# A masked-softmax graph layer on one core: ring transfers of one unit instead of two around the turn between row groups

## What is computed

```python
h = jnp.maximum(_layernorm(x, axis=-1), 0.0)
H = h @ W_fc + b_fc
s_src = H @ w_att[:d]
s_dst = H @ w_att[d:]
scores = s_src[:, None] + s_dst[None, :] + b_att
scores = jnp.where(adj > 0, scores, -1e9)
alpha = jax.nn.softmax(scores, axis=1)
out = x + alpha @ H
```

## Time and profile before

| | us |
|---|---|
| median of three runs | 186.04 |
| lowest, highest | 185.82, 186.31 |
| the profiled execution's own time | 186.24 |
| its span, first to last instruction | 184.3 |
| PE busy | 160.3 |
| DVE busy | 124.9 |
| ACT busy | 79.6 |
| mean rate of the transfers | 389 GB/s |

### The profile page before, as it was taken

One profiled execution on the slowest core, in us unless ns is written; L12 is line 12 of the kernel. 1 busy time (PEld: TensorE's weight loads), 2 busy tenths in 40 slices (PEclk: granted clock), 3 DMA queues, 4 the chain that ended last, 5 costly groups with the idle time before them and its releaser, 6 DMA issues.

```text
span 184.3 us, 2691 instructions
## 1 busy us (share of the span) xinstructions
PE 160.3 (87%) x866; PEld 115.3 (63%) x866; DVE 124.9 (68%) x360; ACT 79.6 (43%) x232; POOL 10.7 (6%) x33
## 2 busy tenths in 40 slices
PE   0639859989499999989899999999999998999970
PEld 0326638666386867656668667686786775887750
DVE  0995696947999556788865569496594624459931
ACT  2567894999395052222251422442224424021020
POOL 2103601000130020000000000000000000000000
PEclk9999987999969999999999999999999999999995
DMA  5999999999999999999999999999999999998212
GB/s 144 410 439 432 412 443 420 434 420 430 427 430 432 412 441 411 441 420 428 420 422 424 427 427 424 422 427 423 425 424 427 437 431 427 411 398 329 76 60 59
DMA packets 8369, 71.63 MB, mean 389 GB/s; under 512 B 929, under 2 KB 1698, under 8 KB 3490
## 3 DMA queue, kind: packets, MB, share of 16 engines
q1 hardware_dynamic: 7776, 71.18, 92.3%
q10 hardware_dynamic: 578, 0.26, 0.5%
HBM read 69.34 MB, written 2.10 MB: 388 GB/s over the span
## 4 chain that ended last, share of the span: by engine, by line
DMA 59%; PE 23%; DVE 10%; issue 2%; ACT 2%; SPq 1%; DVEq 0%
DMA ring<-adj 59%; PE bank L844 9%; PE bank L850 8%; DVE mask L514 5%; PE bank L868 3%; PE bank L892 2%; PE bank L882 1%; DVE low L537 1%; ACT mask L456 1%; DVE mask L523 1%; ACT weighted L363 1%; SPq L271 1%; DVE x_sb L639 1%; DVE x_sb L646 1%; SPq L277 0%
## 5 line engine op out<-in xcount | busy, mean ns | idle before, releaser
L514 DVE TENSOR_SCALAR mask<-ring 128x1024 fp32r<-128x1024 int32 (+2 forms) x69 | 63.1, 934 | 41.6 <-DMA ring<-adj 37.1
L844 PE MATMUL bank<-mask,high 128*128 128x512 f32 x256 | 80.7, 418 | 11.0 <-DVE mask L514 6.3
L850 PE MATMUL bank<-mask,low 128*128 128x512 f32 x256 | 76.3, 401 | 0.0
L844 PEld LDWEIGHTS bank<-mask,high 128*128 128x128 f32 x256 | 47.8, 196 | 31.1 <-DVE mask L514 12.9
L850 PEld LDWEIGHTS bank<-mask,low 128*128 128x128 f32 x256 | 49.8, 194 | 11.1
L456 ACT ACTIVATE mask<-ring,half_steep 128x512 fp32r<-128x512 int32 x43 | 28.9, 718 | 62.1 <-DMA ring<-adj 60.6
L868 PE MATMUL bank<-mask,w_cols 128*32 128x512 bf16 x256 | 19.7, 392 | 2.3 <-ACT lines L422 2.3
L868 PEld LDWEIGHTS bank<-mask,w_cols 128*32 128x32 bf16 x256 | 5.9, 94 | 13.1 <-issue 8.7
L363 ACT ACTIVATE weighted<-relu,w_over_std 128x128 f32<-128x128 f32 x32 | 10.1, 391 | 4.7 <-DVE w_over_std L608 4.5
L374 ACT ACTIVATE relu<-x_sb,neg_mean 128x128 f32<-128x128 f32 x32 | 9.8, 388 | 3.2 <-DVE neg_mean L546 3.2
L389 ACT ACTIVATE high<-x_sb,neg_mean 128x128 fp32r<-128x128 f32 x24 | 9.3, 387 | 0.0
(11 more groups left out here) (85 smaller groups left out, 67.7 us busy)
## 6 DMA issues: line engine op xcount, KB each, us to landing
ring<-adj SPq DMA_DIRECT2D x18, 2048.0 KB, 17.1
ring<-adj SPq DMA_DIRECT2D x16, 1536.0 KB, 12.9
ring<-adj SPq DMA_DIRECT2D x3, 1024.0 KB, 9.3
out<-x_sb SPq DMA_DIRECT2D x7, 256.0 KB, 13.8
x_sb<-x SPq DMA_DIRECT2D x1, 1024.0 KB, 20.7
ring<-adj SPq DMA_DIRECT2D x4, 256.0 KB, 16.2
x_sb<-x SPq DMA_DIRECT2D x2, 256.0 KB, 3.8
x_sb<-x SPq DMA_DIRECT2D x1, 512.0 KB, 10.1
```

The source lines that it names most:

```text
L514: nc.vector.tensor_scalar(mask[:, n % MASKS, 0:cols], ring[:, n // 2 % RING, begin:begin + cols], 0.0, None, ALU.is_gt).then_inc(masks_rea ...
L844: nc.tensor.matmul(bank[:, b, :], high[:, t, :], mask[:, n % MASKS, cols], start=(t == 0), stop=False)
L850: last = nc.tensor.matmul(bank[:, b, :], low[:, t, :], mask[:, n % MASKS, cols], start=False, stop=(t == T - 1))
```

## The change

Eight pairs, 10 to 17 (units 20 to 35; the last six pairs of group 0 and the first two of group 1), come as two transfers of one unit each instead of one of two units. Each half has a semaphore of its own, and the wait for a unit is on its half. The slots of the ring, the condition under which SP may refill a slot, and the order of the work on every engine stay as they are. Both halves of a pair are issued behind the same `slot_free`.

```diff
+HALVED = range(10, 18)
...
+        half_landed = [[sem(f"half_landed{c}_{i}") for i in range(2)] for c in range(RING)]
...
             if pair == 0:
                 engine.wait_ge(first_landed[n], 16)
+            elif pair in HALVED:
+                engine.wait_ge(half_landed[pair % RING][n % 2], 16 * ((pair - HALVED.start) // RING + 1))
             elif n == LAST - 1:
                 engine.wait_ge(next_to_last_landed, 16)
             else:
-                engine.wait_ge(pair_landed[pair % RING], 16 * (pair // RING + (pair % RING > 0)))
+                whole = [p for p in range(1, pair + 1) if p % RING == pair % RING and p not in HALVED]
+                engine.wait_ge(pair_landed[pair % RING], 16 * len(whole))
...
                 if pair >= RING:
                     slot_free(pair)
-                sp.dma_start(ring[:, pair % RING, 0:cols], adj_g[g][t0 // (2 * step)]).then_inc(pair_landed[pair % RING], 16)
+                if pair in HALVED:
+                    for i in range(2):
+                        half = slice(i * cols // 2, (i + 1) * cols // 2)
+                        sp.dma_start(ring[:, pair % RING, half], adj_g[g][t0 // (2 * step)][:, half]).then_inc(half_landed[pair % RING][i], 16)
+                else:
+                    sp.dma_start(ring[:, pair % RING, 0:cols], adj_g[g][t0 // (2 * step)]).then_inc(pair_landed[pair % RING], 16)
```

## The result

The changed kernel takes 186.53 us in the median of 22 runs (185.95 to 187.00), against 185.84 us for the kernel before in 22 runs beside it: a ratio of 1.0032, 95% interval 1.0021 to 1.0043. That is 0.6 us slower (0.4 to 0.8); the two medians alone differ by 0.69. Forecast were +0.62 us and a time of 186.7, with nearly even chances for "within 0.3%" and "slower". The profiled execution took 186.29 us with a span of 184.5, 0.24 under its median; that of the kernel before lay 0.40 over its own, so the two spans are not to be compared to a tenth.

A forecast was written before the change was run, and what follows sets the result against it. The prediction took DMA bytes at a nearly constant rate as the bound, up to pair 32's landing, plus a fixed 29.8 us. Eight splits add 0.62 to 186.04, giving 186.66 us (given as 186.7), range 185.7 to 187.5.

The forecast's parts named there:

- Eight more transfers, +0.62 us: DMA queue: each of eight splits adds one fixed 0.077 us, +0.62 us at pair 32's landing and at the end.
- two steps of the old kernel: Even landing steps, 4.893 us for 2 MiB and 3.689 for 1.5 MiB, giving 0.077 us a transfer plus 2.408 per MiB.
- the last pair (0 for three splits): Lower bound from the stream's end: 1 MiB in four transfers takes 2.5 us, so three further splits cost 0.
- the halves of pair 0 (0.21 a pair): Upper bound from the stream's start: halves landing 2.55 us apart mean 5.1 a pair, +1.7 us for eight.
- Nothing from the earlier starts: At the turn, even units land 2.4 us earlier and slots free sooner, but PE must wait for pair 32: no gain.
- The end is pair 32 plus a fixed 29.8: Group 2: the end is pair 32's landing plus 29.8 us; whatever does not move that landing moves nothing.
- The 1.9 us around the span I leave as they are: Time around the profiled span, taken as unchanged by the added semaphores and changed wait sums.
- A, free pieces: Rival in the DMA stream: packet overhead hides behind the data, the changed kernel takes 186.0 us; chance 0.20.
- B, a starved turn: Rival at pair 25: its 0.97 us delay comes from late issue and would vanish, giving 185.7 us; chance 0.12.
- C, dear halves: Rival in the halved stretch: 8 KB rows at 16 KB stride run like pair 0's halves, +1.7 us, 187.7; chance 0.08.
- D: Rival on PE's clock: smaller heaps of work lower the granted clock, +0.9 us besides the 0.62, 187.6; chance 0.04.

The follow-up runs named there:

- 31 splits: All pairs of groups 0 and 1 (1 to 31) in halves, 31 more transfers than the kernel before: ratio 1.0192, 3.6 us more.
- the tiny transfers: The kernel before with two transfers of 16 rows of 16 bytes behind each of pairs 10 to 17: ratio 1.0018, 0.3 us more.
- The trial by both halves: The changed kernel's halved transfers, but each unit waits for both halves: ratio 1.0057, 1.1 us over the kernel before, 0.5 over the changed one.
- the redundant waits: The kernel before, whole transfers, with one redundant wait ahead of each wait for units 20 to 35 on DVE and ACT: ratio 1.0073, 1.4 us more.
- the last version above: The kernel before with pairs 15, 32, 33 and 34 in halves and DVE's wait for the mean's product one mask later: 184.38 us, ratio 0.9927.
- that cut by partitions: The same eight pairs cut into two transfers of 64 partitions each instead of by columns: ratio 1.1919 to the kernel before, 35 us more.
- the two kernels with added waits: Changed kernel with each unit waiting for both halves, ratio 1.0057; kernel before with a redundant wait for units 20 to 35, ratio 1.0073.

## Why the prediction was right

*Eight more transfers, +0.62 us.* Right in kind and size: 0.56 us by the landings of the halved stretch, 0.070 a split against 0.077, and 0.072 over 31 splits. That pair 32 then landed at 155.13, where 155.1 was foretold, holds 0.13 us of luck: the stream was that much late before the first halved pair. The time of 186.7 stands on a median of three runs that was 0.2 us over that of 22. The price came from two steps of the old kernel that differ only in size. Of its bounds, the last pair (0 for three splits) and the halves of pair 0 (0.21 a pair) are both refuted for this place by the even steps of 2.484, and it was right to take neither. The upper one was a difference of two roundings: unrounded, the halves of pair 0 land 2.49 us apart in the kernel before. The lower one was no rounding, the last unit does come in 2.50 us; it is the stream's end that is different. What the 0.07 is made of I hadn't said; the tiny transfers put most of it on the rows.

*Nothing from the earlier starts.* Right. They brought PE forward at the turn (its product of the mean 0.5 us) and it gave the time back in two waits. SP issued pairs 14 to 19 some 1.3 to 1.7 us sooner, as foretold, but pairs 20 and 21 only 0.2 to 0.3; it made no difference. The trial by both halves looked like a contradiction until the trace put its loss behind the last result, and the redundant waits repeated it without any split.

*The end is pair 32 plus a fixed 29.8.* Right for this change up to the last result, 26.1 us behind the start of pair 32's mask in both kernels, since all of group 2 shifts with the stream. The whole was 29.3 us in the changed kernel's profiled execution and not the same 29.8: what lies behind the last result is not fixed, 3.2 to 4.45 us over these kernels. As a rule it is wrong in a second way: another chain runs from pair 34 over DVE, so what does not move pair 32 can still hold the end. "The 1.9 us around the span I leave as they are" named the wrong piece as the one not seen; the one that moved is the end of the span.

*The rivals.* A, free pieces: refuted, by the step of 4.968 (its sign at the stream's end is real, see above). B, a starved turn: the least time in the queue rose from 10.3 to 11.2 us, pair 24 was issued 0.5 us earlier and lands after 11.5, and pair 25 is late by 0.93 all the same; with more waits in the programs the late step came one pair earlier, at pair 24. In the last version above pair 24 was issued at 109.97 us, 2.5 us earlier than in the kernel before, and pair 25 still came 0.96 late. So it isn't the issue that makes it; what does is open. C, dear halves: refuted, by the same step; rows of 8 KB at a stride of 16 KB gave 0.070 a split where contiguous rows had let expect 0.077, so no price of the stride is seen. D: not in this kernel (granted clock 1.00 through the turn), but seen once PE stood idle 2.67 us. The Trainium skill's 2.0 us for each DMA ("DMA: Bandwidth & Descriptors", Anatomy of one DMA — SWDGE (gpsimd) path), which the page gives for transfers issued by GpSimd, is not what an added transfer on SP's queue costs here, 0.07 us; with 11 us and more from issue to landing, the measurement decides.

## What to carry to other kernels

In a stream that keeps its engines full, a split moves no byte sooner and costs a little, here 0.07 us: split only the transfer for whose *first* part an idle engine waits, and look for the second chain to the end before counting the gain. The marginal price of a transfer can be read from two even steps of different size, better than from any single landing. A difference under 1 us is to be followed in the trace up to the last result, and the stretch behind it read by itself, before it is put down to the edit.

## What was not expected of the hardware

A transfer to 64 neighbouring partitions ran at 216 GB/s where 128 give 425, with the engines' share at 1.00 in both. A few waits more on DVE and ACT, off the path, went with an end of the span of 4.45 us instead of 3.7.

And the stream loses about 1 us twice in each of these kernels, that cut by partitions left out. The second loss, 0.8 to 1.0 us, is at pair 25, and at pair 24 in the two kernels with added waits. The first sums to 0.9 to 1.1 us and lies between pairs 5 and 10: all at pair 9 in the kernel before and the changed one, at pair 5 where each unit waited for both halves, at pair 10 in the last version, split between 5 and 9 with the tiny transfers. With pairs 32 and 34 in halves 0.7 of it came at pair 5, though the transfers ahead of pair 32 are those of the kernel before, so the transfers don't set its place. At the second there is a lead: one packet of 8 KB on the instruction queue q14 moves at 124.6 us in the kernel before, ahead of pair 25's landing, and at 122.0 with the redundant waits, ahead of pair 24's. Yet one at 71.2 us is followed by no late step, so the cause stays open.
